# TensorE's expert pairs 4 to 35 in a loop, and one semaphore for four first sums

## What is computed

```
x = x + tanh(g_xattn) * cross_attention(ctx, layernorm(x))      # 8 heads of 128
x = x + tanh(g_ffn)  * (routed(layernorm(x)) + shared(layernorm(x)))
routed: 8 experts in 2 groups; of the better group the 2 best experts of each token
        y_e = (silu(t @ w_gate[e]) * (t @ w_up[e])) @ w_down[e], weighted and summed
shared: (silu(t @ sw_gate) * (t @ sw_up)) @ sw_down
```

## Time and profile before

| | us |
|---|---|
| median of 3 runs | 1081.3 |
| lowest, highest | 1078.75, 1084.18 |
| the profiled execution, its own time | 1085.61 |
| its span, first to last instruction | 1083.9 |
| attention, about | 0 to 845 |
| shared expert, about | 845 to 905 |
| expert pairs, about | 900 to 1075 |

### The profile page before, as it was taken

One profiled execution on the slowest core, in us unless ns is written; L12 is line 12 of the kernel. 1 busy time (PEld: TensorE's weight loads), 2 busy tenths in 40 slices (PEclk: granted clock), 3 DMA queues, 4 the chain that ended last, 5 costly groups with the idle time before them and its releaser, 6 DMA issues. The chain is left out here.

```text
span 1083.9 us, 24223 instructions
## 1 busy us (share of the span) xinstructions
PE 988.7 (91%) x7050; PEld 934.3 (86%) x7050; DVE 738.6 (68%) x1812; ACT 640.9 (59%) x1550; POOL 488.8 (45%) x774
## 2 busy tenths in 40 slices
PE   5979999999999999999999999999999976677783
PEld 4879999999999999999999999999998865677672
DVE  5756677777777777777777777777776564344552
ACT  5755766667675857676767666676766413234331
POOL 4513233526363635344544535263526653644454
PEclk9998999999999999999999999999999998889897
DMA  9640000000000001010000000000001455764761
GB/s 266 188 161 1 24 4 20 24 21 24 20 23 19 23 19 37 10 37 10 32 15 27 23 19 23 19 23 20 21 1 60 153 199 153 220 192 115 224 179 45
DMA packets 50032, 73.00 MB, mean 67 GB/s; under 512 B 8764, under 2 KB 29231, under 8 KB 49968
## 3 DMA queue, kind: packets, MB, share of 16 engines
q1 hardware_dynamic: 39248, 50.81, 15.7%
q0 software_dynamic: 8064, 21.25, 5.3%
q10 hardware_dynamic: 2656, 0.14, 0.2%
HBM read 39.87 MB, written 33.63 MB: 68 GB/s over the span
## 5 line engine op out<-in xcount | busy, mean ns | idle before, releaser
L430 POOL TENSOR_TENSOR prob<-prob,rinv 128x333 f32<-128x333 f32 x256 | 184.6, 743 | 438.4 <-DVE rinv L961 438.4
L569 ACT ACTIVATE prob<-ps_s,nmax 128x333 f32<-128x333 f32 x256 | 137.5, 537 | 76.0 <-DVE nmax L766 67.2
L766 DVE TENSOR_REDUCE nmax<-ps_s 128x1 f32<-128x333 f32 x256 | 127.1, 497 | 59.5 <-PE ps_s L1087 51.2
L980 DVE TENSOR_TENSOR pt_lo<-ps_t,pt_hi 128x768 fp32r<-128x768 f32 x128 | 122.4, 956 | 26.9 <-ACT pt_hi L598 25.1
L579 ACT ACTIVATE o_hi<-ps_qa,vecs 128x256 fp32r<-128x256 f32 x127 | 60.4, 476 | 97.5 <-PE ps_qa L1087 97.1
L746 DVE SCALAR_TENSOR_TENSOR k_lo<-ps_k,vecs,k_hi 128x334 fp32r<-128x334 f32 x128 | 72.5, 566 | 55.0 <-ACT k_hi L551 54.9
L1087 PE MATMUL ps_qa<-pt_hi,v_hi 128*128 128x256 f32 x381 | 108.7, 285 | 1.2 <-issue 1.2
L1087 PE MATMUL ps_qa<-pt_lo,v_hi 128*128 128x256 f32 x381 | 106.5, 280 | 0.0
L1087 PE MATMUL ps_qa<-pt_hi,v_lo 128*128 128x256 f32 x381 | 106.4, 279 | 0.0
L598 ACT ACTIVATE pt_hi<-ps_t 128x768 fp32r<-128x768 f32 x128 | 104.2, 814 | 3.7 <-PE ps_t L1226 3.3
L1226 PE MATMUL ps_t<-ident,prob 128*128 128x128 f32 (+1 forms) x768 | 105.5, 274 | 0.8 <-POOL prob L430 0.8
(11 more groups left out here) (319 smaller groups left out, 3259.8 us busy)
## 6 DMA issues: line engine op xcount, KB each, us to landing
xin<-by_first SPq DMA_DIRECT2D x21, 260.0 KB
xin<-by_second SPq DMA_DIRECT2D x21, 260.0 KB
xin<-by_first SPq DMA_DIRECT2D x32, 130.0 KB
xin<-by_second SPq DMA_DIRECT2D x32, 130.0 KB
x_all<-in_x_dram SPq DMA_DIRECT2D x1, 3584.0 KB, 18.3
rows_turned<-x2t_hi SPq DMA_DIRECT2D x13, 256.0 KB, 2.1
rows_turned<-x2t_lo SPq DMA_DIRECT2D x13, 256.0 KB, 2.2
w_hi<-rows_turned SPq DMA_DIRECT2D x13, 256.0 KB
```

What stands on the lines that cost most here:

```text
L430: pool.tensor_tensor(prob[:, h % 2, i, 0:KEYS], prob[:, h % 2, i, 0:KEYS], rinv[:, h % 2, i:i + 1].to_broadcast([P, KEYS]), ALU.mult).then ...
L569: act.activation(prob[:, h % 2, i, 0:KEYS], ps_s[i][:, 0:KEYS], ACT.Exp, bias=nmax[:, h % 2, i:i + 1], accum_out=rsum[:, h % 2, i:i + 1]). ...
L766: dve.tensor_reduce(nmax[:, h % 2, i:i + 1], ps_s[i][:, 0:KEYS], AX.X, ALU.max, negate=True).then_inc(max_ready, 1)
L980: dve.tensor_tensor(pt_lo[:, (h - 1) % 2, :], ps_t[:, 0:3 * TOK], pt_hi[:, (h - 1) % 2, :].bitcast(F32), ALU.subtract).then_inc(ptlo_ready, 1)
```

## The change

It has three pieces.

1. PE's loop over pairs. Pairs 0 to 3 and what comes behind pair 35 stay unrolled; pairs 4 to 35 run in a `Fori` of four turns, eight pairs each. Every step (`e_turn_tokens`, `e_gate_up`, `e_turn_hidden`, `e_down_part`) gets two numbers: m, which is known when the program is built and picks buffers and slots, and n = turn + m, a register inside the loop, from which the waits' values are computed. `experts_of` reads the word at an address in a register, and a turn starts by reading again the word of the two pairs that are still in flight. The order of the matmuls stays.
2. So that a slot's semaphore grows by 16 for each use, whatever the tile, the first sums get semaphores of their own: `sum_in[n]`, one for SUMS = 4 tiles, which is awaited at 64 times the rank's count, when all four sums have landed. SP's waits before the sum loads go. PE and ACT wait on `row_in` for 16 times the slot's uses, and DVE for the group's sums (split tiles) or for the slot (others).
3. So that words follow each other over both ranks, tile 37 has the digit behind tile 36: POOL's `affine_select` on `octal` is made in two halves, the second with base 37, and the waits on `octal_set` count one more.

```
-        def fetches(tile):
-            return sum(1 + split_fetch(n) for n in range(tile % NB, tile, NB)) + 1
-
-        def fetches_with_sum(tile):
-            return fetches(tile) + split_fetch(tile)
+        def sum_loaded(tile):
+            rank_no, j = divmod(tile, XTILES)
+            return sum_in[j // SUMS], 16 * SUMS * (rank_no + 1)
...
+            def fetch_sum(tile, start):
+                rank_no, j = divmod(tile, XTILES)
+                sp.dma_start(xin[:, tile % NB, ROW1:PAIR], pairs[rank_no][bass.ds(start, P), ROW1:PAIR])\
+                  .then_inc(sum_in[j // SUMS], 16)
...
                 for tile, start in zip(ahead, starts):
-                    sp.wait_ge(row_in[tile % NB], 16 * fetches(tile))
-                    fetch(tile, start, slice(ROW1, PAIR))
+                    fetch_sum(tile, start)
...
-            pool.affine_select(out=octal[:, :, :], in_=octal[:, :, :], compare_op=ALU.is_equal, fill=0.0, base=0,
-                               pattern=[[-PACK, RANKS * PACKS], [-1, PACK]], channel_multiplier=1).then_inc(octal_set, 1)
+            for n in range(RANKS):
+                part = slice(n * HALF, (n + 1) * HALF)
+                pool.affine_select(out=octal[part, :, :], in_=octal[part, :, :], compare_op=ALU.is_equal, fill=0.0, base=n * XTILES,
+                                   pattern=[[-PACK, RANKS * PACKS], [-1, PACK]], channel_multiplier=1).then_inc(octal_set, 1)
+                pool.wait_ge(octal_set, PACK + 1 + n)
...
-                    dve.wait_ge(row_in[s], 16 * fetches_with_sum(tile))
+                    if split_fetch(tile):
+                        dve.wait_ge(*sum_loaded(tile))
+                    else:
+                        dve.wait_ge(row_in[s], 16 * uses(tile, NB))
...
-            def e_turn_tokens(n):
-                pe.wait_ge(xtlo_ready, LATE + n - 1)
+            def e_turn_tokens(n, m):
+                pe.wait_ge(xtlo_ready, n + (LATE - 1))
                 for i in range(TT):
-                    tile = TT * n + i
-                    pe.wait_ge(row_in[tile % NB], 16 * fetches(tile))
+                    pe.wait_ge(row_in[(TT * m + i) % NB], TT * n + (16 - TT * (m % PER_LOOP)))
...
-            def experts_of(pack):
-                at = P + pack
-                return pe.value_load(tab_row[0:1, at:at + 1], min_val=0, max_val=EXP ** PACK - 1)
+            def experts_of(word):
+                return pe.value_load(tab_row[0:1, bass.ds(word + P, 1)], min_val=0, max_val=EXP ** PACK - 1)
+
+            def expert(word, k_no):
+                return word // EXP ** k_no % EXP
...
+            def e_step(n, m, word, known):
+                tile = TT * m
+                if m < XDUOS:
+                    if tile % PACK == 0:
+                        known["word"] = experts_of(word(tile // PACK))
+                    known[m] = [expert(known["word"], (tile + i) % PACK) for i in range(TT)]
+                if m + 1 < XDUOS:
+                    e_turn_tokens(n + 1, m + 1)
+                if m < XDUOS:
+                    e_gate_up(n, m, known[m])
+                if 0 <= m - 1 < XDUOS:
+                    e_turn_hidden(n - 1, m - 1)
+                if m == 0:
+                    shared_down(DUOS - 1)
+                if m >= 2:
+                    e_down_part(n - 2, m - 2, known.pop(m - 2))
...
+            for n in range(LOOP_N0):
+                if n == 2:
+                    pe.wait_ge(wlo_rest, len(DOWN))
+                e_step(n, n, lambda w: w, known)
+            with pe.Fori(0, LOOP_N1 - LOOP_N0, PER_LOOP) as turn:
+                first = LOOP_N0 - 2
+                word = experts_of(turn // (PACK // TT) + TT * first // PACK)
+                known = {m: [expert(word, (TT * m + i) % PACK) for i in range(TT)] for m in (first, first + 1)}
+                for m in range(LOOP_N0, LOOP_N0 + PER_LOOP):
+                    e_step(turn + m, m, lambda w: turn // (PACK // TT) + w, known)
+            last = LOOP_N1 - 2
+            word = experts_of(TT * last // PACK)
+            known = {m: [expert(word, (TT * m + i) % PACK) for i in range(TT)] for m in (last, last + 1)}
+            for n in range(LOOP_N1, XDUOS + 2):
+                e_step(n, n, lambda w: w, known)
```

More of the change, by code:

```diff
@@ L1297, in sparse_ffn @@
         NB, NY, NR = 16, 7, 5
+        SUMS = 4
+        LOOP_N0, LOOP_N1 = 4, 36
+        PER_LOOP = NB // TT
         FAR_SLOTS = 3
@@ L1391, in sparse_ffn @@
         row_in = [sem(f"x_row_in{s}") for s in range(NB)]
+        sum_in = [sem(f"x_sum_in{n}") for n in range(NB // SUMS)]
         y_sent = [sem(f"x_y_sent{s}") for s in range(NY)]
@@ L1630, in e_address @@
                     s, y = tile % NB, tile % NY
-                    act.wait_ge(row_in[s], 16 * fetches(tile))
+                    act.wait_ge(row_in[s], 16 * uses(tile, NB))
                     if tile >= NY:
@@ L2037, in turn_table, with e_gate_up @@
                   .then_inc(turned_tab, 1)
[L2039 to L2040 removed]
+            def e_turn_tokens(n, m):
+                pe.wait_ge(xtlo_ready, n + (LATE - 1))
                 for i in range(TT):
[L2042 to L2043 removed]
+                    pe.wait_ge(row_in[(TT * m + i) % NB], TT * n + (16 - TT * (m % PER_LOOP)))
                 for c in range(FC):
                     for i in range(TT):
[L2046 to L2047 removed]
+                        mm = pe.transpose(ps_x[:, (LATE + m) % 2, c * TOK + i * P:c * TOK + (i + 1) * P],
+                                          xin[:, (TT * m + i) % NB, HDR + c * P:HDR + (c + 1) * P], ident[:, :])
                 mm.then_inc(x_turned, 1)
[L2050 to L2057 removed]
+            def experts_of(word):
+                return pe.value_load(tab_row[0:1, bass.ds(word + P, 1)], min_val=0, max_val=EXP ** PACK - 1)
+            def expert(word, k_no):
+                return word // EXP ** k_no % EXP
+            def e_gate_up(n, m, which):
+                pe.wait_ge(xtlo_ready, n + (LATE + 1))
+                pe.wait_ge(h_done, n + (DUOS - 1))
+                x_hi, x_lo = k.near_slot(k.w_hi, m % 2), k.near_slot(k.w_lo, m % 2)
                 for i in range(TT):
                     e = which[i]
[L2060 removed]
+                    q = 0
                     for c in range(FC):
@@ L2063, in e_gate_up @@
                         for x, w in ((x_hi, gu_hi), (x_hi, gu_lo), (x_lo, gu_hi)):
-                            mm = pe.matmul(ps_g[:, n % 2, i * TOK:(i + 1) * TOK], x[:, at:at + P],
-                                           w[:, c, bass.ds(e, 1), :].rearrange("p o n -> p (o n)"), start=m == 0, stop=m == 3 * FC - 1)
-                            m += 1
+                            mm = pe.matmul(ps_g[:, m % 2, i * TOK:(i + 1) * TOK], x[:, at:at + P],
+                                           w[:, c, bass.ds(e, 1), :].rearrange("p o n -> p (o n)"), start=q == 0, stop=q == 3 * FC - 1)
@@ L2075, in e_turn_hidden, with e_down_part @@
                 mm.then_inc(h_turned, 1)
-            def e_down_part(n, which):
+            def e_down_part(n, m, which):
                 pe.wait_ge(htlo_ready, n + 1)
-                if n >= 2:
-                    pe.wait_ge(e_y, TT * (n - 1))
+                if m >= 2:
+                    pe.wait_ge(e_y, TT * n - TT)
                 else:
-                    pe.wait_ge(resid_ready, DUOS - 1 + n)
+                    pe.wait_ge(resid_ready, DUOS - 1 + m)
                 for i in range(TT):
-                    for m, (h, w) in enumerate(((ht_hi, dn_hi), (ht_hi, dn_lo), (ht_lo, dn_hi))):
-                        mm = pe.matmul(ps_o[:, n % 2, i * DIM:(i + 1) * DIM], h[:, n % 2, i * P:(i + 1) * P],
-                                       w[:, bass.ds(which[i], 1), :].rearrange("p o n -> p (o n)"), start=m == 0, stop=m == 2)
+                    for q, (h, w) in enumerate(((ht_hi, dn_hi), (ht_hi, dn_lo), (ht_lo, dn_hi))):
+                        mm = pe.matmul(ps_o[:, m % 2, i * DIM:(i + 1) * DIM], h[:, m % 2, i * P:(i + 1) * P],
+                                       w[:, bass.ds(which[i], 1), :].rearrange("p o n -> p (o n)"), start=q == 0, stop=q == 2)
@@ L2109, in _ @@
+            for g in range(DUOS):
+                shared_gate_up(g)
                 if g < LATE:
                     turn_late(g)
-                if DUOS <= g - 1 < UNITS:
-                    e_turn_hidden(g - 1 - DUOS)
-                if 0 <= g - 1 < DUOS:
+                if g >= 1:
                     shared_down(g - 1)
-                if g - 2 >= DUOS:
-                    e_down_part(g - 2 - DUOS, known.pop(g - 2 - DUOS))
                 if 0 <= g - 1 < LATE:
@@ L2122, in _ @@
                     turn_table()
[L2123 to L2126, removed]
+            pe.wait_ge(tab_ready, 1)
+            pe.wait_ge(skip_ready, 1)
+            e_turn_tokens(0, 0)
+            pe.wait_ge(wlo_ready, EARLY - EARLY_LO)
+            known = {}
+            for n in range(LOOP_N0):
[13 more added lines that the diff above has]
+                e_step(n, n, lambda w: w, known)
```

15 lines of the change are left out of this document (8 added, 7 removed).

## The result

The changed kernel took 1086.85 us (median of 5 runs, 1084.92 to 1089.32), the kernel before, measured beside it, 1080.69 us (5 runs, 1077.58 to 1084.18): a ratio of 1.0061, 95% interval 1.0032 to 1.0090, so 6.2 us slower, between 3.5 and 9.7. Forecast were 4.0 us, of which 3.1 came from the sums and 0.9 from table reads. Two later measurements of the same kernel on other chips gave 1.0030 (1.0015 to 1.0045) and 1.0065 (1.0042 to 1.0088).

What follows compares the result with a forecast made beforehand. In the expert part no engine is full and a ring of engines paces it. Sums 3.1, register waits 0, table reads 0.9, code 0 and masks 0 give 4.0 us on 1081.3: 1085.3 us, range 1074 to 1096.

Steps and rivals of the forecast that it cites:

- Sums in groups of four: At both rank starts DVE waits for four sums, delaying outputs, w_lo and PE: 3.1 us, bounds 0 to 4.
- Later groups: Sum groups 1 to 3, issued 2.1 to 6.3 us later than group 0 but wanted later still: no cost.
- Table reads: On PE's sequencer, 15 reads instead of 10, 0.18 us showing for each: 0.9 us, bounds 0 to 2.3.
- register waits: Nine wait calls a pair on PE now compare computed values: taken as 0, at most 14.7 us for 32 pairs.
- loop ends: Four compare-and-branches on PE of 0.208 us each: taken as 0, at most 0.8 us.
- The prediction's reason: In the expert part the ring leaves PE 0.5 us in each 8.14 us beside 22.1 us of waits, hiding register work.
- Code loading: On PE's code queue in the expert part, about seven of ten 16 KB packets fall away: taken as 0.
- the rival that had the removed packets in the stalls: In the expert part, seven removed code packets each take away an ht_lo wait: faster, 1071 or 1078 us; chance 0.16.
- Masks: On POOL one affine_select of 0.41 us becomes two, at most 0.5 us more, taken up by later scatter slack: 0.
- SP's removed waits save nothing: On SP, one wait for each of 32 sum loads goes; loads already followed at 0.52 us, so no gain.
- 3.6 to 3.9 us behind the first sum issue: Sign of being right: DVE's first output of each rank this far behind, instead of 2.1 to 2.3 us.
- The shorter ht_lo waits: Sign of being right: PE's waits for DVE's ht_lo, 22.1 us in 11, shorten by what register work fills.

Runs made afterwards that it cites:

- the exchange: An edit on VectorE (DVE) putting w_lo of pairs 4 and 22 ahead of each rank's first outputs; kernels with it measured 0.9975 to 1.0014 of the kernel before.
- hoist_loop: The changed kernel (loop, groups of four) with w_lo of pairs 4 and 22 ahead of the first outputs on VectorE: 1083.29 us, 1.0014 of the kernel before.
- a third pair: The changed kernel with each of TensorE's nine waits a pair issued three times, looped against unrolled: 1092.48 and 1090.12 us, both 1.0096 of the kernel before.
- a fourth: Sums grouped 1, 1, 4, 10 with w_lo ahead of first outputs, looped against unrolled: 1081.55 and 1078.23 us, 1.0010 and 0.9975 of the kernel before.
- sums_only: The changed kernel with TensorE's loop unrolled again, sums still in groups of four: 1089.97 us, 1.0030 of the kernel before.
- hoist_fine_unrolled: The changed kernel unrolled, sums grouped 1, 1, 4, 10, w_lo of pairs 4 and 22 ahead of first outputs: 1078.23 us, 0.9975 of the kernel before.
- the first chip: Runs of the changed kernel, looped and unrolled, with groups of four (1090.37, 1089.97 us) and with groups 1, 1, 4, 10 (1085.62, 1084.94 us).
- waits3_unrolled: The changed kernel with TensorE unrolled and each of its nine waits a pair issued three times against constants: 1090.12 us, 1.0096 of the kernel before.

## Why the prediction was right, and where a term was off

- **Sums in groups of four, forecast 3.1 us:** right in place and mechanism, shown by unrolling (no change), by regrouping (the cost goes) and by a longer group (it grows, and PE's waits for w_lo with it). That it goes through the order on VectorE is read from the traces; the exchange bears it out only in part, since *hoist_loop* recovers something and the groups still cost with it. The size was off: 4.75 and 5.03 us. The step that failed is "with the same landing time both starts move by 1.57 and 1.56 us". In rank 1 it nearly holds, 1.5 to 1.9 us. In rank 0 the first output moved by 2.0 to 3.0 us (4.27 to 5.27 for 2.30): the fourth load was issued up to 2.35 us behind the first in a trace instead of 1.58, and it landed and was used up to 3.68 us after its issue. The token loads that SP issues until just before it (x14 until 918.98 us in the changed kernel, the first sum at 919.31) may be why; that wasn't tested. My bound of 4 us named "a busy queue" and was still too low.
- **Later groups, nothing:** nothing speaks against it; after the rank starts the time for four outputs doesn't go by the grouping (7.19 to 7.98 us with groups of four and single waits, 7.69 to 8.12 with the first sum alone and no exchange).
- **Table reads, 0.9 us, register waits and loop ends, nothing:** the loop cost 0.4 and 0.7 us on one chip, nothing in a third pair and 3.8 us in a fourth, both of these across chips. The count of 15 reads and 4 branches was right. The nine computed waits a pair were not nine more instructions of 51 ns: the sequencer has 136 more register and wait instructions in all from 900 to 1070 us, about four a pair, and the register steps take 32 to 46 ns. That the ring hides such work is right for most of it and not all: 327 more wait instructions cost some 3.5 us. The prediction's reason was misread: the 0.5 us between PE's last gate-and-up matmul and ACT's SiLU is that of one pair in the earlier trace rows, and in 14 of the 37 pairs of the same trace the SiLU starts less than 0.1 us behind that matmul, whose end is modelled. At those PE has no slack that the trace shows.
- **Code loading, nothing:** right; 4 packets for 10, no packet per turn, and 9 packets in sums_only with no loss. The first of the four turns ends at 962.9 us, and behind 965 us the code queue brings nothing up to 1063 us. So a jump back reloads nothing, and the rival that had the removed packets in the stalls stands only if a cost of register work cancels its gain. The rule from the Trainium skill's "Runtime: NRT & Kernel Launch", section "Instruction fetch mechanics", that a taken branch beyond a two-page window forces a load, did not show in these turns, by the prediction's estimate of 2.2 packets and somewhat more each.
- **Masks, nothing:** 0.88 us for 0.41. Not tried alone; four variants that share them and have a semaphore for the first sum alone lie at 0.9985 to 1.0010 of the kernel before, and hoist_fine_unrolled at 0.9975, so they cost little or nothing.
- **SP's removed waits save nothing:** open, between 0 and some 2 us gained.
- **What would show it:** "3.6 to 3.9 us behind the first sum issue" was missed in rank 1 of the predicted trace (4.06) and held in rank 1 of all further ones with groups of four (3.64 to 3.78); rank 0 lay above it throughout (4.27 to 5.27). PE's waits of "5.7 to 6.1" came as 5.11 and 7.03. The shorter ht_lo waits came, but also in the unrolled sums_only (14.8 us for 22.1), so register work isn't what filled them; that reading of mine was wrong.
- **The sum:** 1085.3 forecast, 1086.85 measured. The groups (4.75 to 5.03), the loop's cost on the first chip (0.4 to 0.7) and a gain of 1.5 us or nothing on the rest add up to 3.7 to 5.7 us; the three comparisons gave 6.2, 3.2 and 7.0. The forecast of 4.0 us is near them partly by luck: the groups were put 1.7 to 1.9 us too low and the table reads 0.2 to 0.5 us too high. The shared expert's part before the first sum ended 2.1 us later in the trace of after; in the other traces it lies at 915.9 to 919.4 us with and without the loop, so it is taken for spread and not for a cost.

## What to carry to other kernels

A semaphore shared by a group makes its first user wait for the last member. Price it as the steps of issue plus the landing in the queue's busiest stretch, not in a quiet one, and look at what stands behind the waiting instruction on its engine. If semaphores are short, spend them on the first members (1, 1, 4, 10) and not evenly: that took the whole cost away, looped and unrolled. Where the waiting engine also feeds the bottleneck, putting that feed ahead of the wait is worth a try: it kept TensorE from standing idle and its clock up at one start, but what it brought at the end ranged from 1.7 us or more to nothing. Only two versions here have intervals below the kernel before, both unrolled and with a semaphore for the first sum alone: with the exchange (0.9975, 0.9962 to 0.9989) and without it (0.9985, 0.9974 to 0.9997). Rolling a loop up cost under 1 us in three of four pairs on an engine that waits a fifth of the time (24.0 of 30 us busy), and here it gained nothing either.

## What the runs showed of the hardware that I had not expected

A wait instruction on PE's sequencer takes 51 ns at the median, but beside bursts of scatters the same instructions can take 0.70 us each (700 and 712 ns at most in the rows of waits3_unrolled). While GpSimd issued eight scatters in a row there, 1.28 us apart, from 940.12 to 949.08 us, the gate-and-up at 946.66 started 1.76 us late with no releaser (timelines of PE's weight loads and of POOL):

```profile
946.66 0.19 PEld L2081 LDWEIGHTS ps_g<-w_hi 128*128 128x128 f32 x1 [1.76 <-issue]
```

```profile
941.40 0.98 POOL L1559 DMA_INDIRECT by_second<-late,to_late  x1 [0.31 <-issue]
...
946.52 0.98 POOL L1559 DMA_INDIRECT by_second<-late,to_late  x1 [0.30 <-issue]
```

Of the sequencer's register, wait and table-read instructions between 900 and 1070 us, 2 of 624 took over 0.4 us in the kernel before, 5 of 760 in the changed one and 27 of 946 in waits3_unrolled, three of these being real waits of 1.5 to 6.6 us. It is no steady count: two further traces of the changed kernel have 12 and 4. More instructions on a waiting engine may get their price there; that, and whether the scatters cause it, was not tried.
